# A mixture-of-experts stage: combine weights spread by DMA from the third chunk on, its sum turned instead of folded, and a residual addition moved to GpSimd

## The reference, cut to what matters

```python
h = h + _L1_ffn_ref(_layernorm(h, axis=-1), router_w, w1, b1, w2, b2)
# with tokens = the normed h:
probs = softmax(tokens @ router_w.T); rw, re = top_k(probs, 2); rw = rw / rw.sum(-1)
combine = zeros((N, 8)).at[arange(N)[:, None], re].set(rw)
out = tokens
for e in range(8):
    y = gelu(tokens @ w1[e] + b1[e]) @ w2[e] + b2[e]
    out = out + combine[:, e:e + 1] * y
```

## Time and profile before

| | before |
|---|---|
| median of 3 runs | 736.25 us (734.73 to 738.40) |
| profiled execution | 734.71 us, span 732.9 us |
| PE / DVE / ACT / POOL busy over the span | 87% / 78% / 68% / 47% |
| PE, DVE, ACT busy in 700 to 710 us | 10.00, 4.85, 4.94 of 10 us |
| PE, DVE, ACT busy in 690 to 700 us | 7.89, 5.15, 5.08 of 10 us |
| second experts, first `hidden(0,1)` to last addition | 665.6 to 727.8 us |

### The profile page before, as it was taken

How to read it: one execution, slowest core, us unless ns; L and a number is a source line. 1 busy time by engine, 2 the same in 40 slices (tenths; PEclk the granted TensorE clock), 3 DMA queues, 4 the chain that set the end, 5 groups by cost and what they waited for, 6 DMA issues and landing times.

```text
span 732.9 us, 16305 instructions
## 1 busy us (share of the span) xinstructions
PE 635.8 (87%) x4928; PEld 352.1 (48%) x4928; DVE 570.1 (78%) x1627; ACT 501.6 (68%) x1264; POOL 345.1 (47%) x431
## 2 busy tenths in 40 slices
PE   5526998999999998989999996799888888889896
PEld 5514665666666654222222225456555555564332
DVE  6676787777777784899999989679988898867653
ACT  2746877888888873576777777567777777744542
POOL 1005678778788775333444445625444644320000
PEclk9959999999999999999999998699999999987999
DMA  4030000000000000533333330000000000000011
GB/s 111 1 115 1 1 2 1 0 0 0 0 0 0 0 1 30 191 116 116 106 116 117 115 117 2 1 1 2 1 0 0 0 0 0 1 1 0 16 22 22
DMA packets 22421, 24.36 MB, mean 33 GB/s; under 512 B 12390, under 2 KB 13414, under 8 KB 22118
## 3 DMA queue, kind: packets, MB, share of 16 engines
q1 hardware_dynamic: 20135, 23.31, 10.2%
q10 hardware_dynamic: 2239, 0.49, 0.4%
HBM read 22.48 MB, written 1.31 MB: 32 GB/s over the span
## 4 chain that ended last, share of the span: by engine, by line
PE 53%; DVE 25%; issue 9%; ACT 3%; POOL 2%; DMA 2%; SPq 0%; DVEq 0%; ACTq 0%; POOLq 0%
PE ps L726 8%; PE ps L762 7%; DVE big L1103 5%; PE ps L1571 5%; PE ps L1593 4%; PE ps L720 4%; DVE big L2082 3%; DVE big L1144 3%; PE ps L1577 2%; DVE big L1053 2%; PE ps L708 2%; PE ps L1822 2%; PE ps L1844 2%; PE ps L712 2%; PE ps L1583 1%
## 5 line engine op out<-in xcount | busy, mean ns | idle before, releaser
L1358 POOL TENSOR_TENSOR big<-big 128x1024 f32<-128x1024 f32 x64 | 119.8, 1893 | 45.6 <-DVE big L1164 45.6
L942 ACT ACTIVATE big<-ps,big 128x255 f32<-128x255 f32 x256 | 117.3, 484 | 11.1 <-DVE big L1158 8.6
L904 ACT ACTIVATE big<-ps,b1s 128x512 f32<-128x512 f32 x128 | 80.8, 682 | 29.3 <-PE ps L644 28.2
L1158 DVE TENSOR_REDUCE big<-ps 128x4 f32<-128x1020 f32 x64 | 75.2, 1213 | 25.5 <-PE ps L720 25.5
L1940 ACT ACTIVATE big<-ps 128x1024 f32<-128x1024 f32 x64 | 65.9, 1030 | 33.0 <-PE ps L1583 30.5
L2082 DVE TENSOR_REDUCE big<-ps 128x4 f32<-128x1020 f32 x64 | 78.1, 1220 | 6.8 <-DVE res L2139 2.5
L726 PE MATMUL ps<-cst,big 128*128 128x128 f32 x512 | 76.7, 283 | 6.3 <-POOL big L1358 2.4
L1170 DVE COPY mid<-ps 128x512 f32<-128x512 f32 x96 | 63.4, 686 | 18.3 <-PE ps L726 15.0
L726 PEld LDWEIGHTS ps<-cst,big 128*128 128x128 f32 x512 | 54.2, 140 | 40.8 <-issue 21.5
L644 PE MATMUL ps<-big,wall 64*128 64x512 f32 x256 | 72.1, 640 | 0.4 <-ACT big L875 0.4
L655 PE MATMUL ps<-big,w2s 128*64 128x512 f32 x256 | 69.0, 616 | 2.8 <-DVE big L1144 2.4
(11 more groups left out here) (277 smaller groups left out, 1322.7 us busy)
## 6 DMA issues: line engine op xcount, KB each, us to landing
mid<-spread_w SPq DMA_DIRECT2D x128, 128.0 KB, 2.9
mid<-in_split_sel SPq DMA_DIRECT2D x1, 1536.0 KB, 8.7
wall<-in_w SPq DMA_DIRECT2D x1, 1280.0 KB, 7.2
out_tokens<-res SPq DMA_DIRECT2D x16, 56.0 KB, 1.6
cst<-in_consts SPq DMA_DIRECT2D x1, 520.5 KB, 5.0
pexp<-in_w_raw SPq DMA_DIRECT2D x1, 512.0 KB, 6.0
w2s<-in_w SPq DMA_DIRECT2D x1, 512.0 KB, 3.4
mid<-in_taps ACTq DMA_DIRECT2D x1, 320.0 KB, 4.0
```

What stands on the lines that cost most here:

```text
L904: last = nc.scalar.activation(hid[e % 2][j], H1(e, j), ACT.Relu, bias=b1s[0][:, 2 * e + j:2 * e + j + 1])
L942: last = nc.scalar.activation(e_sb[r % 4][:, jj, tq, 0:NW], S[:, 2 * (r % 2) + jj, tq, 0:NW], ACT.Exp, scale=-1.0, bias=minus[r % 4][:, jj ...
L1158: nc.vector.tensor_reduce(minus[r % 4], S[:, 2 * a:2 * a + 2, :, 0:NW], AX.X, ALU.min).then_inc(s_mx, 1)
L1358: nc.gpsimd.tensor_tensor(e_sb[r % 4], e_sb[r % 4], bc(inverse[r % 4].unsqueeze(3), [P, 2, 2, 256]), ALU.mult).then_inc(s_A, 1)
```

## The change

Chunks 0 and 1 keep the matmul spread (`BY_PE = 2`). For chunks 2 to 7 the fp32 combine weights are turned once per half (`combine_turn(n)` on TensorE into bank 5, `combine_out(n)` on ScalarE), written to `spread_w`, and read back by SyncE, each expert's row 64 times, into eight buffers (`by_dma`, the space of `pos_t`). `weigh` then multiplies two SBUF operands. `sum_turn` becomes four fp32 turns of 128x128, and `finish` adds the two halves from PSUM; GpSimd adds the normed tokens to `res` ahead. To have the second half's weights early, `combine(1)` and `gap(1)` move forward: VectorE now runs `best(7)` and `difference(1)` ahead of `weigh(1,0)`, and `combine(1)` ahead of `weigh(1,1)`. `weights(4..7)` move from chunk 3 to chunk 2. SyncE's loop of stores is written out, with the spreading transfers between the stores.

```diff
+                def combine_turn(n):
+                    pe.wait_ge(s_comb, CH + n + 1)
+                    if n == 0:
+                        pe.wait_ge(s_lc, 5)
+                    else:
+                        pe.wait_ge(s_wgt, GROUPS * BY_PE)
+                    nc.tensor.transpose(ps[:, 5, 0:P], comb_rows[n], ident).then_inc(s_cwp, 1)
...
                     for k in range(TC):
-                        last = nc.tensor.matmul(YT[:, D * k:D * k + D], y_sb[:, P * k:P * k + P], fold[:], start=True, stop=True)
+                        last = nc.tensor.transpose(YT[:, P * k:P * k + P], y_sb[:, P * k:P * k + P], ident)
...
                     weights(d)
+                combine_turn(0)
                 for c in range(CH):
                     hidden(c, 1)
...
-                    spread(c, 0)
+                    if c < BY_PE:
+                        spread(c, 0)
                     if c >= 1:
                         second(c - 1, 1)
...
-                    if c == 3:
-                        pe.wait_ge(s_wgt, GROUPS * c + 1)
+                    if c == BY_PE:
+                        pe.wait_ge(s_cw, CH + 2)
                         for d in range(4, CH):
                             weights(d)
...
-                    spread(c, 1)
+                    if c < BY_PE:
+                        spread(c, 1)
                     if c >= 1:
                         sum_turn(c - 1)
+                    if c == 1:
+                        combine_turn(1)
...
+                def combine_out(n):
+                    act.wait_ge(s_cwp, CH + n + 1)
+                    nc.scalar.activation(comb_turned[n], ps[:, 5, 0:P], ACT.Copy).then_inc(s_cw, 1)
...
+                        if g == 1 and c == 1:
+                            gap(1)
                         if g == 0 and c == 2:
-                            gap(1)
-                        if g == 0 and c == 3:
+                            combine_out(1)
                             for d in range(4, CH):
                                 weights(d)
...
-                    link(nc.vector.tensor_tensor(yy, y, x2[:, tl, 0], ALU.add))
-                    nc.vector.tensor_tensor(res[:, tl], res[:, tl], yy, ALU.add).then_inc(s_done, 1)
+                    dve.wait_ge(s_pre, c + 1)
+                    link(nc.vector.tensor_tensor(yy, halves[:, 0], res[:, tl], ALU.add))
+                    nc.vector.tensor_tensor(res[:, tl], yy, halves[:, 1], ALU.add).then_inc(s_done, 1)
...
                     for n in range(2):
-                        last = nc.vector.tensor_tensor(wgt[2 * g + n], hid[2 * g + n], CB(n), ALU.mult)
+                        slot_of = 4 * (c % 2) + 2 * g + n
+                        if c >= BY_PE:
+                            dve.wait_ge(s_by_dma[slot_of], spread_before[slot_of] + 32 * (c // 2))
+                        last = nc.vector.tensor_tensor(wgt[2 * g + n], hid[2 * g + n], CB(n) if c < BY_PE else by_dma[slot_of], ALU.mult)
...
                 weigh(0, 1)
-                weigh(1, 0)
                 best(7)
                 difference(1)
+                weigh(1, 0)
+                combine(1)
                 weigh(1, 1)
                 finish(0)
                 for c in range(2, CH):
                     weigh(c, 0)
-                    if c == 2:
-                        combine(1)
                     weigh(c, 1)
                     finish(c - 1)
...
+                for c in range(CH):
+                    pool.wait_ge(s_nx, 2 * c + 2)
+                    tl = slice(TC * c, TC * c + TC)
+                    nc.gpsimd.tensor_tensor(res[:, tl], res[:, tl], x2[:, tl, 0], ALU.add).then_inc(s_pre, 1)
...
-                with sp.Fori(0, CH) as c:
-                    store(c)
+                def spread(c):
+                    n, row = c // (CH // 2), c % (CH // 2)
+                    for k in range(2 * GROUPS):
+                        slot_of = 4 * (c % 2) + k
+                        if c >= BY_PE + 2:
+                            sp.wait_ge(s_wgt, GROUPS * (c - 2) + k // 2 + 1)
+                        for j in range(2):
+                            e = 2 * k + j
+                            sp.dma_start(by_dma[slot_of][D * j:D * j + D], bc(there[n][4 * e + row:4 * e + row + 1], [D, 512])).then_inc(s_by_dma[slot_of], 16)
+                for n in range(2):
+                    sp.wait_ge(s_cw, CH + n + 1)
+                    sp.dma_start(there[n].rearrange("(e c) (t q) -> (e c t) q", e=E, t=TC), comb_turned[n]).then_inc(s_there, 16)
+                    sp.wait_ge(s_there, 16 * (CH + n + 1))
+                    for c in ((2, 3), (4, 5))[n]:
+                        spread(c)
+                for c in range(2):
+                    store(c)
+                for c in range(6, CH):
+                    spread(c)
+                    store(c - 4)
+                for c in range(4, CH):
+                    store(c)
```

More of the change, by code:

```diff
@@ L1447, in attention0_and_experts0 @@
             later.s_hid, later.s_m, later.s_w2, later.s_tot, later.s_fin, later.s_e0_nx = s_hid, s_m, s_w2, s_tot, s_fin, s_e0_nx
+            later.s_cb, later.s_comb, later.s_ctp, later.s_ct = s_cb, s_comb, s_ctp, s_ct
             later.s_cd, later.s_tr, later.s_selb, later.s_pexp, later.duos = s_cd, s_tr, s_selb, s_pexp, DUOS * CH
@@ L1530, in attention1_and_experts1 @@
             small_work = lambda first, n: mid[:, first:first + n * NT].rearrange("p (t e) -> p t e", t=NT)
-            lg, comb = small_work(4608, E), small_work(4864, E)
+            lg = small_work(4608, E)
+            comb_rows = [mid[:, 4864 + P * n:4864 + P * n + P] for n in range(2)]
+            comb = [rows.rearrange("p (e t) -> p t e", e=E) for rows in comb_rows]
+            comb_turned = [big[:, 11008 + P * n:11008 + P * n + P] for n in range(2)]
+            BY_PE = 2
+            by_dma = [pos_t[:, n].rearrange("p c q -> p (c q)") for n in range(H)]
+            there = [spread_w[2 * n:2 * n + 2].rearrange("c e q -> (c e) q") for n in range(2)]
             v8, pick = small_work(5136, E), small_work(5392, E)
@@ L1546, in attention1_and_experts1 @@
             s_ysb, s_yt, s_done, s_out = (sem("e1_" + n) for n in ("sum_in_sbuf", "sum_turned", "added", "stored"))
+            s_comb, s_cwp, s_cw, s_there = e0.s_comb, e0.s_ctp, e0.s_ct, e0.s_cd
+            s_by_dma, s_pre = e0.s_cb + [sem(f"e1_spread{n}") for n in range(4, H)], sem("e1_tokens_added")
+            spread_before = [32 * (e0.duos // 4)] * 4 + [0] * 4
             def at(k):
@@ L1830, in spread @@
                         pe.wait_ge(s_lc, 5)
+                    if s == 0:
+                        pe.wait_ge(s_cw, CH + 1)
                     if s >= 1:
@@ L1898, in _ @@
                         logits(6 + c)
-                    spread(c, 1)
+                    if c < BY_PE:
+                        spread(c, 1)
                     if c >= 1:
                         sum_turn(c - 1)
+                    if c == 1:
+                        combine_turn(1)
                     if c == 0:
                         pe.wait_ge(s_ct, 4)
+                    elif c == 4:
+                        pe.wait_ge(s_ct, CH)
                     second(c, 0)
@@ L2045, in _ @@
                     weights(d)
+                combine_out(0)
                 for c in range(CH):
@@ L2235, in combine @@
                     shape = [P, half, E]
-                    where = lambda dst, i: nc.vector.tensor_tensor(dst[:, tl], bc(iota[:, 0:E].unsqueeze(1), shape), bc(idx[:, tl, i].unsqueeze(2), shape), ALU.is_equal)
-                    link(where(comb, 0))
-                    link(where(pick, 1))
+                    where = lambda dst, i: nc.vector.tensor_tensor(dst, bc(iota[:, 0:E].unsqueeze(1), shape), bc(idx[:, tl, i].unsqueeze(2), shape), ALU.is_equal)
+                    link(where(comb[n], 0))
+                    link(where(pick[:, tl], 1))
                     dve.wait_ge(s_ex, n + 1)
@@ L2243, in combine @@
                     link(nc.vector.tensor_tensor(wts[:, 3, tl], wts[:, 0, tl], wts[:, 2, tl], ALU.mult))
[L2244 to L2248, removed]
+                    for i, dst in ((0, comb[n]), (1, pick[:, tl])):
+                        link(nc.vector.tensor_tensor(dst, dst, bc(wts[:, 2 + i, tl].unsqueeze(2), shape), ALU.mult))
+                    nc.vector.tensor_tensor(comb[n], comb[n], pick[:, tl], ALU.add).then_inc(s_comb, 1)
+                    dve.wait_ge(s_comb, CH + n + 1)
+                    thrice = lambda a: bc(a.unsqueeze(2), [P, half, 3, E])
                     hi, md, lo = (c3[:, tl, :, E * n:E * n + E] for n in range(3))
@@ L2251, in combine @@
                         dve.wait_ge(s_pad3, 1)
[L2252 to L2255, removed]
+                    link(nc.vector.tensor_copy(hi, thrice(comb[n])))
+                    link(nc.vector.tensor_tensor(pick[:, tl], comb[n], hi[:, :, 0], ALU.subtract))
+                    link(nc.vector.tensor_copy(md, thrice(pick[:, tl])))
```

(20 more changed lines are left out.)

## The result

| | before | after |
|---|---|---|
| first comparison, median of 4 runs each | 735.49 us (733.83 to 738.40) | 743.46 us (742.49 to 747.44) |
| repeated later, 25 and 10 runs | 735.72 us (732.40 to 740.51) | 742.00 us (738.10 to 748.31) |
| profiled execution, span | 734.71, 732.9 us | 742.49, 740.7 us |
| `hidden(0,1)` to the end of the last addition | 665.6 to 727.80: 62.2 us | 663.8 to 735.83: 72.0 us |

A forecast was written before the change was run, and what follows sets the result against it. TensorE, without a gap in chunks 4 to 6, was taken as the bound. Stage -3.4 plus clock 2.0 made -1.4: 733.3 us against the profiled 734.71, 734.9 us against the median 736.25; range 732.0 to 739.0.

The forecast's parts named there:

- Transfers: SyncE's queue, chunks 2 to 7: 5.4 us of issues per chunk against 4.94, kept up by starting ahead; no cost.
- Hidden, with 1.8 us in hand: Chunk 7's spreading transfers land at 718.0, before weigh needs them at 719.8; each us of landing beyond that costs one.
- My own sign of being wrong: Weigh waiting for a DMA in chunks 4 to 7, chunks over 5.2 us, or no pause in chunk 1.
- Transfers late: Rival: SyncE's 5.4 against 4.94 and landing 1 us longer in chunks 6 and 7, about +1.1, 736.0; chance 0.10.
- The clock: TensorE's clock falls in chunk 1's two pauses; 4 us low after 687.3 costs 2.0 us, bounds 0 and 6.2.
- Clock stays low: Rival: low-clock work behind 687.3 lasts beyond 6.8 us, +2.8, 739.1; chance 0.15.
- The plain count: Rival: chunk 1's order costs nothing, so spreads and turns save 10 us, 726.3; chance 0.05.
- The bare chunk of 4.94 us: Chunks 4 to 6 stay bound by TensorE at 4.94 us each, 14.8 instead of 19.3 in all.
- the order of chunks 1 to 3: TensorE waits 2.9 and 4.1 us in chunk 1; chunks 1 to 3 take 27.1 us instead of 25.2.
- the tail of 8.6: From hidden(7,1) at 715.8 to the end of the last addition at 724.4, instead of 727.8.
- the turned sum: Sum_turn as four fp32 turns takes 0.59 us, so 0.45 us goes in each chunk.
- GpSimd at nothing: GpSimd's eight additions, from near 669, end by 686 even at 2.12 us each, before finish at 687.3; no cost.

The follow-up runs named there:

- late traffic: The changed kernel with the spreading transfers of chunks 2 and 3 held back until weigh(0,1) is done; 741.42 us, ratio 1.0057.
- split kernel: The changed kernel with stores of chunks 0 to 5 on GpSimd's queue, 6 and 7 on SyncE's; 736.52 us, ratio 1.0003, repeated 735.71 us.
- stores on GpSimd's queue: The changed kernel with all 32 stores issued from GpSimd's queue, so SyncE issues only spreads; 745.68 us, ratio 1.0092.
- old order alone: The changed kernel with weigh(1,0) ahead of best(7), combine(1) in chunk 2, second-half weights turned in chunk 3; 738.86 us, ratio 1.0044.
- split with old order: The changed kernel with stores 0 to 5 on GpSimd's queue and VectorE's and ScalarE's order as before the change; 734.14 us, ratio 0.9961.

## Why the prediction was wrong

**Transfers: the step that failed.** I put 0.5 us on an issue, 0.36 on a store and 2.9 on the landing, and found them "Hidden, with 1.8 us in hand". My own sign of being wrong came true: `weigh` waits for a DMA in chunks 6 and 7. Measured were 0.64 (10.29 for 16), 0.52 to 0.58 (2.06 for four, 4.67 for eight) and 3.7 for the last. From the copy of half two (`combine_out(1)`) to the last landing my sum ran from 691.7 to 718.0, 26.3 us. It took from 698.55 to 727.52 + 3.73 = 731.25: 32.7. `weigh(7,1)` could have started some 28 us behind that copy, at 719.8 in the sum and at 723.20 + 4.0 = 727.2 here. So the place was right and the direction was a rival, "Transfers late", but at +1.1 instead of +5. Nor did its +1.1 follow from my sum: a landing 1 us longer stays within the 1.8 us in hand. The reason is in how I read the earlier trace rows: 469 ns is the median of 128 issues spread over 146 us, most of them 0.8 to 0.9 us apart. The trace of the kernel before held the price of a row as well, in the first sixteen of these very transfers:

```profile
289.38 10.46 SPq L1429 DMA_DIRECT2D mid<-spread_w  x16
```

10.46 / 16 = 0.65 us. I took a price from transfers that were seldom back to back for a queue that I had myself found over its capacity (5.4 against 4.94). With 0.64 and 0.55 it is 8 x 0.64 + 4 x 0.55 = 7.3 us of SyncE per chunk against 4.94, and no start ahead lasts for six chunks. Moving the stores takes the loss away (6.3 us on one chip). The profiles of the changed kernel show 4.7 and 6.0 us of it (the second: chunk 6 from 722.25 to 727.98, tail to 741.82, against 4.94 and 8.6), that of the late traffic 5.9.

**The clock: right for the pauses, blind for the start.** That a fall comes with the pauses is shown: in all six profiles with the new order a stretch at 0.50 of 10 to 11 us begins between 683 and 694 (of the two with the old order, one has none there and one has one from 692 on). Each time it begins within 1.2 us of the end of the first pause and ahead of the second, so one pause of 3.1 us stands before it and not two. Behind the second pause 3.5 us of it are left in the changed kernel and 4.6 to 4.9 in the split one; I had taken 4. Its price in the split kernel, chunk 1 at 16.5 and chunk 2 at 8.0 against 14.8 and 7.1, is 2.6, of which 0.4 is `combine(1)` (in the changed kernel 686.82 to 691.10, 4.28 us against the 3.88 of my sum); I had put 2.0 on it. What I left out is that the low stretch that was there already, the 12.5 us of the earlier trace rows, could reach into the stage. In the profiled execution it lasted to 682.4, and chunks 0 and 1 took 11.8 + 19.6 = 31.4 us where the split kernel, with a rise near 671, took 8.0 + 16.5. Of these 6.9 us not all is lost against other executions, since this one had reached the stage 4.6 us earlier than the split kernel's.

*What stays open* is why this first stretch lasts 13 to 17 us in some executions and 30 to 31 in others. It was long in both profiles of the changed kernel and in those of two variants (stores on GpSimd's queue, old order alone), short in four (both profiles of the split stores, split with old order, late traffic) and in all five whose stage starts as before. Traffic alone is excluded, and so is a gap on TensorE (19.00 of 19.00 us busy). The place of the stores does not decide it either: it was long with no store on SyncE's queue and short with all of them there (late traffic), one profile each. Three of the four long ones are the longest run of their kernel (748.31, 749.2 and 749.87 us), so the medians need not hold it. The mean granted clock over the span was 0.94 in the median of 14 runs of the changed kernel, 0.946 in 20 of the split one, and 0.955 in the 25 of before beside the last of them. Part of the difference between the first two lies in the tail, where the changed kernel's profiles end with 7.1 and 11.5 us at 0.50 and the split one's with 1.6 and 1.8. How the 6.3 us divide between waits and clock is therefore shown only by the profiles: 4.7 to 6.0 us of waits.

**The rivals.** "Clock stays low" gave 739.1 for the wrong stretch: low work beyond 6.8 us behind the pauses. The second stretch ended at 696.0, within that, and what was low for long lay ahead of the pauses. The Trainium skill's rule on turns (TensorE: Matmul & The Clock Gate, Part 4: PE-mode transpose), which would have drawn that case out, shows no effect here: from 706 to 718 each chunk holds four turns, and the clock stays at 1.00.

```profile
706.00:718.00 12.00, 12.00 (x54) 4.01 (x55) 7.86 (x15) 7.72 (x14) 0.00 (x0) 1.00 0.58 153
```

That is a mild test, since the turns take 0.6 of the 4.9 us of a chunk. Two of my readings for that rival were loose: of the 3.09 us of the earlier trace rows only 1.4 lie ahead of the rise at 450.2 (other turns fill the rest of that stretch), and the 12.5 us of the earlier trace rows also hold eight 512-column matmuls, those of `hidden(0,0)` and `hidden(0,1)`. "The plain count" (726.3) fell with the pauses of 3.1 and 3.5 us, where I had put 2.9 and 4.1.

**What held.** The bare chunk of 4.94 us, the order of chunks 1 to 3 with each wait and its releaser, the tail of 8.6 once nothing is late, the turned sum, and GpSimd at nothing (eight additions in 5.50 us from 666.91, long ahead of the first `finish`). The products with both operands in SBUF took 0.69 us (a pair 1.29).

## What to carry to other kernels

Before a queue is given more transfers, add up its issues in order, at the price of back-to-back ones, and compare with the time of the stage that uses them: a median over scattered issues is the lower end. Put what nobody waits for (stores) behind what somebody waits for, or on another queue; only the last stores are better left where the kernel ends sooner behind them (5 us on SyncE's queue, 8.7 on GpSimd's). A forecast that holds piece by piece can still miss by what it borrowed from an idle neighbour, so the resource that is first found near its limit deserves the wide bound, not a reserve of 1.8 us.

## What the runs showed of the hardware

An issue of 64 repeated rows (128 KB) on SyncE's queue took 0.47 us when the issues were 0.8 to 0.9 us apart and 0.60, 0.64 with the gap, in a row; the stores behind them took 0.46 instead of the 0.33 of the earlier trace rows. Four stores took 2.40 us to issue on GpSimd's queue and 2.06 on SyncE's, and with the last four on GpSimd's the end came 8.7 us behind the last addition instead of 5. The granted clock stayed at 0.50 for 30.6 us of which TensorE was busy for 29.5 (changed kernel, 651.7 to 682.3), and over the 14 runs of the changed kernel each further us at the lower level goes with 0.30 us of time (a line fitted to span and mean clock of each run; the correlation is 0.85).
